# Attention row shifts transposed by VectorE instead of TensorE, and a retimed order of the whole program, in a fused FFN, attention, FFN kernel

## The reference

```python
x = x + 0.5 * ffn(layernorm(x))
x = x + attn(layernorm(x))          # q, k, v = proj(x); rope; softmax(q k^T / 4 + causal mask) v; @ Wo.T
x = x + 0.5 * ffn(layernorm(x))     # ffn(x) = (silu(x Wg^T * gs) * (x Wu^T * us)) Wd^T * ds, 704 inner columns
```

## Time and profile before

| | before |
|---|---|
| median of three runs | 888.81 us |
| the profiled execution: its time, its span | 890.0 us, 888.2 us |
| TensorE busy, share of the span | 845.6 us, 95% |
| VectorE, ScalarE, GpSimd busy | 643.0, 557.7, 376.8 us |
| mean granted clock of TensorE | 0.984 |

### The profile page before, as it was taken

How to read it: one execution, slowest core, us unless ns; L and a number is a source line. 1 busy time by engine, 2 the same in 40 slices (tenths; PEclk the granted TensorE clock), 3 DMA queues, 4 the chain that set the end, 5 groups by cost and what they waited for, 6 DMA issues and landing times.

```text
span 888.2 us, 17639 instructions
## 1 busy us (share of the span) xinstructions
PE 845.6 (95%) x6426; PEld 565.2 (64%) x6426; DVE 643.0 (72%) x1273; ACT 557.7 (63%) x1096; POOL 376.8 (42%) x355
## 2 busy tenths in 40 slices
PE   7999999999999999999989999999999999999996
PEld 6788888775654555555545566454554546888885
DVE  5767678876989988688889878788878902655442
ACT  4765645355567767556847565777567876665652
POOL 1758685453243434151243441321231324656553
PEclk9999999998999999899979999999999999999999
DMA  9701233008265165352443716432641111001001
GB/s 320 287 1 72 84 95 107 4 13 218 75 181 172 49 171 146 121 163 76 91 127 131 195 37 159 111 97 67 199 111 40 39 52 32 29 24 44 30 24 50
DMA packets 61956, 89.80 MB, mean 101 GB/s; under 512 B 14892, under 2 KB 27564, under 8 KB 61612
## 3 DMA queue, kind: packets, MB, share of 16 engines
q1 hardware_dynamic: 61724, 88.57, 33.9%
q10 hardware_dynamic: 144, 0.07, 0.0%
HBM read 45.52 MB, written 40.76 MB: 97 GB/s over the span
## 4 chain that ended last, share of the span: by engine, by line
PE 77%; DVE 12%; ACT 5%; issue 3%; DMA 1%; POOL 1%; SPq 1%; DVEq 0%; POOLq 0%; ACTq 0%
PE psum L860 14%; PE psum L971 13%; PE psum L923 11%; PE psum L954 10%; PE psum L830 10%; PE psum L886 9%; PE psum L839 5%; DVE NP L1203 5%; PE psum L933 2%; DVE ST L1111 2%; ACT XN L1012 2%; PE psum L846 2%; ACT PT L1083 2%; DVE HF_f L1154 1%; DMA X<-x 1%
## 5 line engine op out<-in xcount | busy, mean ns | idle before, releaser
L1203 DVE TENSOR_REDUCE NP<-psum 128x1 f32<-128x512 f32 (+3 forms) x640 | 363.6, 627 | 68.8 <-PE psum L933 50.6
L1083 ACT ACTIVATE PT<-psum 128x512 f32<-128x512 f32 (+2 forms) x640 | 307.9, 568 | 155.2 <-PE psum L954 153.5
L1299 POOL TENSOR_SCALAR_AFFINE_SELECT PT<-PT 128x512 f32<-128x512 f32 x128 | 80.7, 638 | 229.8 <-ACT PT L1083 176.7
L954 PE MATMUL psum<-Q,K 50*128 50x512 f32 (+2 forms) x768 | 142.3, 411 | 7.3 <-ACT PT L1083 4.5
L860 PE MATMUL psum<-XH,WG_f 128*128 128x512 f32 x352 | 142.6, 405 | 5.9 <-DVE HF_f L1154 5.1
L923 PE MATMUL psum<-K,Q 48*128 48x512 f32 (+2 forms) x768 | 144.5, 406 | 3.6 <-DVE NP L1203 1.3
L971 PE MATMUL psum<-PT,V 128*32 128x512 f32 (+3 forms) x1536 | 146.2, 499 | 0.7 <-ACT PT L1083 0.5
L860 PE MATMUL psum<-XL,WG_f 128*128 128x512 f32 x352 | 138.5, 393 | 0.0
L1256 POOL TENSOR_TENSOR HL_f<-HF_f,HH_f 128x512 fp32r<-128x512 f32 x80 | 102.9, 1296 | 79.8 <-ACT HH_f L1041 79.8
L1154 DVE SCALAR_TENSOR_TENSOR HF_f<-psum,US,G_f 128x512 f32<-128x512 f32 x96 | 71.2, 750 | 64.7 <-PE psum L860 29.0
L923 PEld LDWEIGHTS psum<-K,Q 48*128 48x128 f32 x768 | 69.8, 187 | 64.9 <-DVE NP L1203 25.1
(11 more groups left out here) (77 smaller groups left out, 1081.2 us busy)
## 6 DMA issues: line engine op xcount, KB each, us to landing
zd<-ZH SPq DMA_DIRECT2D x32, 512.0 KB, 4.6
Q<-zd SPq DMA_DIRECT2D x64, 192.0 KB, 3.8
K<-zd SPq DMA_DIRECT2D x64, 192.0 KB, 4.9
zd<-ZL SPq DMA_DIRECT2D x16, 512.0 KB, 5.1
od<-OS SPq DMA_DIRECT2D x32, 256.0 KB, 2.6
OC<-od SPq DMA_DIRECT2D x32, 128.0 KB
SC<-rd_ SPq DMA_DIRECT2D x32, 128.0 KB
out<-X SPq DMA_DIRECT2D x16, 256.0 KB, 2.1
```

The costliest lines, as they stand in the source:

```text
L954: ins = tn.matmul(dst, K[k][r, p, j * P:(j + 1) * P], Q[k][r, p, 512 * c2 + base:512 * c2 + 512], start=True, stop=True)
L1083: sc.activation(dst, src, ACT.Exp, scale=0.25).then_inc(S["act_exp"], 1)
L1203: ve.tensor_reduce(out=acc, in_=src, axis=AX, op=ALU.max, negate=True).then_inc(S["dve_max"], 1)
L1299: gp_.affine_select(out=pt, in_=pt, compare_op=ALU.is_ge, fill=0.0, base=0, pattern=[[0, 4], [1, P]], channel_multiplier=-1).then_inc(S["p ...
```

## The change

1. `pe_nT` and `act_nt` go. VectorE transposes `NM` in 32x32 blocks into `NMT`, now 128 by 32, as a last step of `dve_nm`, behind a wait on its own step before. The write to DRAM puts the four blocks in place.
2. The play's durations change: `MODE_NS` gets a fourth kind, "mask" (a `pe_s` with mask products), a form of the array of its own in cost though not in choice (`ARRAY`), a TensorE that stood idle pays `RELOAD_NS`, and the costs of `pe_s`, `pe_st`, `pe_pv` and `dve_nm` and the shares `BUSY` are set anew.

No other instruction changes its shape. The number of `pe_warm` in the play goes from 188 to 221, of which 133 before and 168 after stand between the last `pe_dn` of the first layer and the first `pe_g` of the second, in 92 and 123 runs of neighbours.

```diff
-MODE_NS = {("full", "half"): 190, ("col", "half"): 110, ("half", "full"): 30, ("half", "col"): 30, ("full", "col"): 60, ("col", "full"): 60}
+MODE_NS = {("full", "half"): 170, ("col", "half"): 105, ("half", "full"): 175, ("half", "col"): 117, ("full", "col"): 70, ("col", "full"): 70,
+           ("half", "mask"): 23, ("mask", "half"): 82, ("full", "mask"): 186, ("col", "mask"): 126, ("mask", "full"): 214, ("mask", "col"): 145,
+           ("mask", "mask"): 103}
+RELOAD_NS = 90
...
-BUSY = {"full": 0.92, "half": 0.8, "col": 1.0}
+BUSY = {"full": 0.92, "half": 0.85, "mask": 0.75, "col": 0.95}
+ARRAY = {"full": "full", "half": "half", "mask": "half", "col": "col"}
...
-                        if self.mode[piece] != mode[0]:
-                            ns += MODE_NS[mode[0], self.mode[piece]]
-                            mode[0] = self.mode[piece]
+                        change = MODE_NS.get((mode[0], self.mode[piece]), 0)
+                        ns += max(change, RELOAD_NS * (free[e] < now))
+                        mode[0] = self.mode[piece]
...
-            add(key, 350 + 150 * c2, "dve_nm", gr, c2, after=drained + ([("pe_nT", gr - 2, c2)] if gr >= 2 else []))
-            add(key, 120, "pe_nT", gr, c2, after=[("dve_nm", gr, c2)], room=(1,))
             was = (gr - 1, c2)
-            add(key, act_ns(P) + 20, "act_nt", gr, c2, after=[("pe_nT", gr, c2)] + ([turn_of("nw", *was)] if gr else []), empties=[("pe_nT", gr, c2)])
-            add(key, 600, *turn_of("nw", gr, c2), after=[("act_nt", gr, c2)] + ([turn_of("nm", *was)] if gr else []))
+            add(key, 450 + 150 * c2, "dve_nm", gr, c2, after=drained + ([turn_of("nw", *was)] if gr else []))
+            add(key, 600, *turn_of("nw", gr, c2), after=[("dve_nm", gr, c2)] + ([turn_of("nm", *was)] if gr else []))
...
-                    w = sum({0: 865, 128: 652, 256: 438, 384: 250}[e_skip(c2, i)] for i in (j - 1, j))
+                    w = 94 + sum({0: 865, 128: 652, 256: 438, 384: 250}[e_skip(c2, i)] for i in (j - 1, j))
...
-                    ve.tensor_tensor(shift_parts(gr, c2, 1), src, f32(shift_parts(gr, c2, 0)), ALU.subtract).then_inc(S["dve_nm"], 1)
+                    ve.tensor_tensor(shift_parts(gr, c2, 1), src, f32(shift_parts(gr, c2, 0)), ALU.subtract).then_inc(S["dve_nl"], 1)
+                    e.wait_ge("dve_nl", *a)
+                    if gr:
+                        e.wait_ge(*turn_of("nw", gr - 1, c2))
+                    both = f32(NM[gr % 2][:, c2, :, :, :, :]).rearrange("p a b c t -> p (a b c t)")
+                    ve.transpose(NMT[c2][:, :], both).then_inc(S["dve_nm"], 1)
...
-                    sy.dma_start(NMD[c2], f32(NMT[c2][:, :])).then_inc(sem, 16)
+                    sy.dma_start(NMD[c2].rearrange("r (k n) -> k r n", k=4), NMT[c2][:, :]).then_inc(sem, 16)
```

More of the change, by code:

```diff
@@ L76, in raises @@
     return [(kind, 1)]
-EMPTIES = {"act_exp": "act_out", "act_o": "act_out", "act_v": "act_out", "act_nt": "act_out", "act_xh": "act_out", "act_qk": "act_out",
+EMPTIES = {"act_exp": "act_out", "act_o": "act_out", "act_v": "act_out", "act_xh": "act_out", "act_qk": "act_out",
            "act_silu": "act_out", "dve_max": "dve_out", "dve_rope": "dve_out", "dve_xl": "dve_out", "dve_h": "dve_out", "dve_t2": "dve_out",
            "dve_xo": "dve_out"}
-INNER = {"dve_va": ("dve_bn", "dve_ag"), "dve_nm": ("dve_mn", "dve_nh"), "pool_r": ("pool_ts", "pool_tc"), "dve_flagint": ("dve_flagsum",)}
+INNER = {"dve_va": ("dve_bn", "dve_ag"), "dve_nm": ("dve_mn", "dve_nh", "dve_nl"), "pool_r": ("pool_ts", "pool_tc"), "dve_flagint": ("dve_flagsum",)}
 DMAS = {"dma_ld": 4, "dma_zw": 3, "dma_nm": 2, "dma_oc": 2, "dma_on": 2, "dma_sp": 2, "dma_w2": 2}
@@ L198, in choose @@
                 kind = item[2][0]
-                cost = item[0] + (0 if self.mode[item[2]] == mode[0] else MODE_PLACE) - URGE.get(kind, (0,) * 9)[held.get(kind, 0)]
+                cost = item[0] + (0 if ARRAY[self.mode[item[2]]] == ARRAY[mode[0]] else MODE_PLACE) - URGE.get(kind, (0,) * 9)[held.get(kind, 0)]
                 if best is None or (cost, item) < best[:2]:
@@ L284, in settle @@
             later = [free[e] for e in self.order if free[e] > now and (ready[e] or e == "PE" and todo)] + [x[0] for x in ends]
-            if todo and free["PE"] <= now:
+            if todo and ends and free["PE"] <= now:
                 later.append(now + 100)
@@ L491, in maxima @@
                 done += n
[L492 to L495, removed]
+                sets = 2 if u == "a" else 1
+                add(key, sets * (max(s_width(t, ch), 256) * 0.4167 + (26 if ch < c2 else 80)), "pe_s", *unit, after=[ld(gr, ch), ld(gr, c2), ("act_mk",)],
+                    room=(2,), mode="half" if ch < c2 else "mask")
                 for hh in range(2):
@@ L520, in heads @@
             was = pt_before(gr, c2, j)
-            add(key, (2 if u == "a" else 1) * (max(512 - skip, 256) * 0.443 + 40), "pe_st", *unit,
+            add(key, (2 if u == "a" else 1) * (max(512 - skip, 256) * 0.4167 + (14 if u == "a" else 26)), "pe_st", *unit,
                 after=([was] if was else ffn1_end) + [ld(gr, c2), ld(gr, j // 4), turn_of("nm", gr, c2), (f"dma_on{gr % QK}",)],
@@ L661, in macaron @@
         NM = [place(f"NM{i}", [P, 2, 2, 2, 2, 4], F32R) for i in range(2)]
-        NMT = [place(f"NMT{i}", [32, P], F32R) for i in range(2)]
+        NMT = [place(f"NMT{i}", [P, 32]) for i in range(2)]
         SU, RC = ([place(f"{n}{i}", [P, 16]) for i in range(2)] for n in ("SU", "RC"))
@@ L934, in tensor_program @@
                     ins.then_inc(S["pe_s"], 1)
[L935 to L940, removed]
                 elif kind == "pe_st":
@@ L1213, in vector_program @@
                         e.wait_ge("dve_mn", *a)
-                    if gr >= 2:
-                        e.wait_ge("pe_nT", gr - 2, c2)
                     src = np_[:, 0, t, :].rearrange("p t (a b) -> p t a b", a=2)
@@ L1394, in sync_program @@
                     gr, c2 = a
-                    e.wait_ge("act_nt", *a)
+                    e.wait_ge("dve_nm", *a)
                     if gr:
                         e.wait_ge(*turn_of("nm", gr - 1, c2))
-                    sy.dma_start(NMD[c2], f32(NMT[c2][:, :])).then_inc(sem, 16)
+                    sy.dma_start(NMD[c2].rearrange("r (k n) -> k r n", k=4), NMT[c2][:, :]).then_inc(sem, 16)
                 elif name[:2] == "nm":
```

6 lines of the change are left out of this document (removed).

## The result

The changed kernel takes 916.38 us, median of four runs (913.57 to 917.45), beside 889.89 us of the kernel before: a ratio of 1.0297, 95% interval 1.0266 to 1.0328. It is slower by 26.5 us where I had forecast 883 us and a range up to 898.

A forecast was written before the change was run, and what follows sets the result against it. TensorE's list was taken as the bound (77% of the chain). Terms -7.1 - 3.8 - 5.9 - 1.0 + 9.2 + 1.5 + 1.2 = -5.9 us on 890.0 gave 884.1, forecast as 883 us; own range 876 to 889, overall 866 to 898.

The forecast's parts named there:

- The transposes: TensorE's list: 32 transposes of the shifts go, 14 at 0.46 us and 18 at 0.04; 7.1 us won.
- the time won turns into waits for banks: Rival: VectorE and ScalarE set the pace where no `pe_pv` stands; 0 us won, 889 us; chance 0.14.
- The waits that go: TensorE's waits ahead of the transpose of the shifts, 7.6 us in total; half counted, 3.8 us won, bounds 0 to 7.6.
- The clock: Three low-clock holes mid-span: first goes, half of the others, times 0.77; 5.9 us won, bounds 0 and 9.2.
- Holes of the clock at other places: Sign of being wrong: low-clock stretches elsewhere in the span, with about 12 us missing as before.
- The `pe_warm` that come: Between the feed-forward layers, 35 more unread products in 31 more runs; 55% of 16.6, 9.2 us lost, bounds 4 and 16.6.
- the order of the rest: TensorE's list without `pe_warm` and transposes: 355 changes of form for 338, 17 x 0.09; 1.5 us lost.
- The new step of VectorE: VectorE's 32 block transposes at 0.22 us, possibly held by GpSimd; 1.2 us lost on the path, at most 7.0.
- What costs nothing: ScalarE's lost copies, the rewritten write of the shifts and SyncE's queue, moved by single places: no cost counted.
- The slower rival: Attention, between `pe_st` and `pe_s`: added whole-array products paid in full, late banks keep the holes; +12.6 us, 901 us, chance 0.24.

The follow-up runs named there:

- The kernel with the order of before: Kernel before, its order kept on every engine, the 32 shift transposes moved from TensorE to VectorE: 1.005 of the kernel before.
- the one with its own order: Kernel before with only the transposes moved to VectorE, old durations, order played anew: 0.9989 of the kernel before.
- the changed kernel with its two copies moved: Changed kernel with two `act_lh` ten places later on ScalarE and the GpSimd step behind each three places later: 902.51 us, 1.0121 of the kernel before.
- the tables alone: Kernel before with only the play's new durations and rule of choice, transposes still on TensorE: 1.0267 of the kernel before.

## Why the prediction was wrong

**The transposes (7.1 us won).** The work went, the time didn't. The kernel with the order of before lost 0.5%, the one with its own order stayed at 0.9989. The rival "the time won turns into waits for banks" fits this part: TensorE's waits grew by 4.5 us in the first of the two. No run takes the transposes away and changes nothing else, so their price of 7.1 us isn't measured by itself.

**The waits that go (3.8 won).** The mechanism I gave was right: GpSimd holds VectorE's small steps, and banks stay late. VectorE and GpSimd of the changed kernel ahead of the hole at 360 us show it again:

```profile
355.06 0.17 DVE L1204 CAST NM<-NP 128x16 fp32r<-128x16 f32 x1
355.26 2.40 DVE L1206 TENSOR_TENSOR NM<-NP,NM 128x16 fp32r<-128x16 f32 x1
357.70 0.21 DVE L1211 STREAM_TRANSPOSE NMT<-NM 128x32 f32<-128x32 f32 x1
```

```profile
355.24 2.38 POOL L1284 TENSOR_TENSOR ZL<-TR,ZH 128x1024 fp32r<-128x1024 f32 x1 [0.24 <-ACT ZH L1043]
357.57 1.27 POOL L1298 TENSOR_TENSOR OC<-OC,SC 128x512 f32<-128x512 f32 x1
```

A step of 0.19 us takes 2.40, as long as GpSimd's ZL, and TensorE then waits 1.61 us for a maximum, where before it waited for the shifts:

```profile
352.26 0.28 PE L940 MATMUL psum<-IDT,NM 128*32 128x128 f32 x1 [1.67 <-DVE NM L1219]
```

The hole at 360 us is thus the old one of 352 us, behind another wait of the same size. I should have counted 0, the end of my own bound.

**The clock (5.9 won).** Wrong in sign, and the largest error. I asked of each old hole whether its cause goes, and took it that none would come. The order as a whole was new, and so were the engines' waits: 29 us of clock missing for 14 in the profiled executions. The hole at 200 us did shrink, from 3.4 us of missing clock to 1.7. The wait there, of which I had counted 1.0 us as won, did not: TensorE waits 2.43 us at 202.18 where it waited 2.11. The two largest holes, with their waits, cost some 15 us. "Holes of the clock at other places" was one of my own signs of being wrong.

**The `pe_warm` that come (9.2 lost).** Direction right, size uncertain still: 13.2 us for 31 where they were added to the kernel before, nearer my upper bound of 16.6 than 9.2, but 5.2 us for 35 where they were taken away from the changed kernel with its two copies moved. The 1.5 us for the order of the rest no run isolates.

**The new step of VectorE (1.2 lost).** The duration was right: 212 ns each for the 220 assumed, and it is not held. The pair of fences above shows one that ran beside GpSimd's OC, 357.70 to 357.91. All 32 lie between 211 and 215 ns, while L1206 goes up to 2399. What the step costs on the path no run shows; the kernel with the order of before, which has it too, lost 4.4 us. The Trainium skill (SBUF — State Buffer, "SBUF: two separate sides") makes the lock depend on two SBUF inputs or a two-port mode. By that rule the transpose, with one input, takes no lock unless it runs in such a mode, and the trace agrees with no lock. One input alone doesn't decide it: the rounding, with one input too, is held, here beside a ZL from 249.64 to 252.00:

```profile
251.03 1.01 DVE L1204 CAST NM<-NP 128x16 fp32r<-128x16 f32 x1
```

**What costs nothing.** This is the step that failed beside the clock's: I had looked at where the pieces of SyncE moved, and wrote that the queue "is otherwise moved by single places". By the lists, 59 of its 290 pieces moved by two to five places, and the largest move stands just ahead of the late scale. Its order, ScalarE's, and GpSimd's have to be read against each other. ScalarE's list from OH to OS at 432 us was the same as before, and at 582 us only one half of an exponential had moved from between them to ahead of OH; what OH waited for came later, and in this trace it cost TensorE 5.3 us of waiting, and with the holes behind some 15, where I had counted nothing. The write of the shifts costs SyncE 0.55 us in place of 0.34, and a `pe_st` that waits for the shifts' transfer, which I had excluded, shows in six of the experiments, with 1.7 to 5.0 us, though not in the changed kernel; one of the six still has TensorE's transposes, so the new form of the write isn't needed for it.

**The slower rival (901 us, 0.24).** Even this case was 15 us short. It had the sign and, by the 31 products added, their price, yet not the main mechanism. The account that the runs give, in the order in which things were taken away from 26.5 us: 15.7 for the two waiting copies, 5.2 for 35 products, and 5.6 left (0.63%). The first is shown well, by ratio and by place; the second is known only to 2 to 8 us, and the third with it. The kernel with the order of before and VectorE's transposes is slower by 4.4 us (0.50%), so the rest may be the transposes' own, but that is an argument from two similar numbers. The terms aren't independent: the same 35 products without the two copies moved gave nothing measurable.

**What stays open.** Why the new durations lead to orders with long waits isn't settled: the tables alone (1.0267) and the changed kernel with old unit costs (1.024) are nearly as slow with other waits at other places. The two waiting copies are shown as the cause of their two holes by moving them, but that SyncE's new order is what made them wait is read from the traces alone. Whether the late scale itself would be harmless with ScalarE's and GpSimd's lists left alone wasn't tried in a form that moved SyncE by one place only.

## What to carry to other kernels

Where a change makes the play choose a new order, price the new order and not the edit: read, for each long wait of the old trace, which pieces on the other engines protect the places that have none, and reckon with new waits of the same size as the old. Here two waits of TensorE of 2.7 and 2.6 us cost some 15 us together through the clock behind them, and it was enough to move the instruction that stood at the head of ScalarE's queue and waited, through GpSimd, for a DMA. Work that fills TensorE's gaps is to be tried with less of it, since its price is what the next wait and the clock leave of it.

## What the runs showed of the hardware

- VectorE's transpose of 128x32 float32 in 32x32 blocks takes 212 ns (211 to 215 in 32), also while a GpSimd operation with two inputs runs (357.70 and 510.29 us in the changed kernel); a subtraction of 128x16 in the same chain took 191 ns at the median and 2399 at the most, a rounding of 128x16 with one input 182 and 1010.
- In the changed kernel five TensorE waits of 0.97 to 2.68 us were each followed by a stretch of 8 to 16 us with a mean clock of 0.57 to 0.68, and with two of the waits gone their stretches had 1.00. Such a wait is not always followed by one: behind 1.56 us at 313.93 in the kernel with the order of before, behind 1.15 us at 253.66 in the changed kernel with 35 products fewer, and behind 0.98 us at 712.25 in the kernel before, the clock of the next 8 us was 1.00.
- A lone 128x128 whole-array product among half-array pieces cost 0.43 us when 31 were added, and gave back 0.11 when 63 were taken away.
- A write of 16 KB issued by SyncE occupied its queue for 0.55 us with 128 partitions of 128 bytes, and 0.34 us with 32 rows of 512.
